# Two transformer layers on one core: weights split in pieces, context handed over by features, and another order of slots in the second pass

## The reference, cut to what matters

```
# layer 0
t1 = layer_norm(x) ; x = x + attn(t1, t1, mask) @ Wo.T + bo
x  = x + (context @ Wg.T + bg)
x  = x + relu(layer_norm(x) @ W1.T + b1) @ W2.T + b2
# layer 1
x  = x + mha(layer_norm(x), layer_norm(x), causal)
y  = x + mha(layer_norm(x), context)
z  = layer_norm(y) ; out = y + relu(z @ w1 + b1) @ w2 + b2      # 16 heads of 16 features
```

## Time and profile before

| | us |
|---|---|
| median of 3 runs | 1629.85 (1628.0 to 1630.69) |
| the profiled execution, its own time | 1625.86 |
| its span | 1624.1 |

### The profile page before, as it was taken

One profiled execution on the slowest core, in us unless ns is written; L12 is line 12 of the kernel. 1 busy time (PEld: TensorE's weight loads), 2 busy tenths in 40 slices (PEclk: granted clock), 3 DMA queues, 4 the chain that ended last, 5 costly groups with the idle time before them and its releaser, 6 DMA issues.

```text
span 1624.1 us, 39350 instructions
## 1 busy us (share of the span) xinstructions
PE 1448.7 (89%) x13568; PEld 1184.2 (73%) x13568; DVE 1193.5 (73%) x3871; ACT 1033.5 (64%) x2089; POOL 835.1 (51%) x1125
## 2 busy tenths in 40 slices
PE   2799999999999999878887888888999999999986
PEld 2578888888888888765665656656777777777766
DVE  3788878888888887767777677787677776777642
ACT  3677777777777775555666656666666566665652
POOL 4455544545555565544434444545565555656533
PEclk8899999999999999989999999999999999999999
DMA  4554433443344443444454454554344433344200
GB/s 134 163 147 120 120 105 105 116 121 105 112 117 124 125 124 92 131 124 135 113 144 124 112 146 120 158 145 117 97 111 119 117 100 103 105 119 123 79 20 13
DMA packets 163605, 187.07 MB, mean 115 GB/s; under 512 B 15953, under 2 KB 140241, under 8 KB 163409
## 3 DMA queue, kind: packets, MB, share of 16 engines
q1 hardware_dynamic: 163408, 184.57, 40.1%
HBM read 125.78 MB, written 58.72 MB: 114 GB/s over the span
## 4 chain that ended last, share of the span: by engine, by line
PE 59%; ACT 15%; DVE 14%; issue 8%; POOL 2%; DMA 1%; SPq 1%; DVEq 0%; ACTq 0%; POOLq 0%
PE d_ps L451 23%; PE d_ps L713 8%; PE o_ps L587 8%; PE s_ps L509 6%; PE t_ps L523 6%; DVE prob L915 4%; ACT prob_t L761 4%; PE t_ps L557 3%; ACT q_stack L769 3%; PE m_ps L458 3%; ACT xt_hi L776 1%; ACT h_f L853 1%; DVE top L900 1%; DVE stats L921 1%; DVE q_part L1017 1%
## 5 line engine op out<-in xcount | busy, mean ns | idle before, releaser
L761 ACT ACTIVATE prob_t<-t_ps 128x384 f32<-128x384 f32 (+1 forms) x512 | 275.7, 550 | 354.8 <-PE t_ps L557 189.3
L509 PE MATMUL s_ps<-k_stack,q_stack 96*128 96x256 bf16 (+1 forms) x1536 | 288.9, 270 | 81.0 <-DVE top L915 50.1
L752 ACT ACTIVATE prob<-prob,neg_max 128x256 f32<-128x256 f32 x512 | 233.5, 509 | 115.3 <-DVE neg_max L915 113.1
L509 PEld LDWEIGHTS s_ps<-k_stack,q_stack 96*128 96x128 bf16 x1536 | 116.1, 99 | 175.9 <-issue 68.2
L557 PE MATMUL t_ps<-q_stack,k_stack 108*128 108x256 bf16 (+1 forms) x1024 | 205.5, 267 | 29.8 <-ACT prob_t L761 27.4
L1137 POOL TENSOR_TENSOR h_lo<-h_f,h_hi 128x512 fp32r<-128x512 f32 x128 | 164.9, 1288 | 119.8 <-DVE h_hi L1032 119.8
L915 DVE CUSTOM_DVE_ANT_0 prob<-s_ps,bias_sb 128x256 f32<-128x256 f32 x512 | 193.3, 418 | 30.3 <-PE s_ps L509 29.8
L900 DVE TENSOR_REDUCE top<-s_ps 128x2 f32<-128x512 f32 x256 | 172.6, 682 | 46.8 <-PE s_ps L509 43.3
L915 DVE CUSTOM_DVE_ANT_0 prob<-s_ps,causal 128x128 f32<-128x128 f32 (+1 forms) x512 | 157.4, 352 | 54.5 <-PE s_ps L509 52.9
L587 PE MATMUL o_ps<-prob_t,v_sb 128*17 128x256 f32 (+1 forms) x3072 | 195.4, 373 | 0.0
L451 PE MATMUL d_ps<-x2t_hi,w_hi 128*128 128x256 f32 x512 | 156.6, 306 | 15.3 <-ACT k_f L834 10.3
(11 more groups left out here) (127 smaller groups left out, 4051.2 us busy)
## 6 DMA issues: line engine op xcount, KB each, us to landing
parts<-q_part SPq DMA_DIRECT2D x96, 192.0 KB, 2.3
parts<-k_part SPq DMA_DIRECT2D x96, 192.0 KB, 2.3
q_stack<-parts SPq DMA_DIRECT2D x96, 192.0 KB, 3.3
k_stack<-parts SPq DMA_DIRECT2D x96, 192.0 KB, 3.3
q_stack<-parts SPq DMA_DIRECT2D x96, 128.0 KB, 3.1
k_stack<-parts SPq DMA_DIRECT2D x96, 128.0 KB, 3.2
ct_kept<-ct_hl SPq DMA_DIRECT2D x16, 512.0 KB, 3.5
x_in<-x_mid SPq DMA_DIRECT2D x32, 256.0 KB, 3.0
```

The costliest lines, as they stand in the source:

```text
L509: last = mm(s_ps[:, h % 2, q * S:q * S + n], q_stack[0:ROWS, t.par, head_of(t, h), q * P:(q + 1) * P], k_stack[0:ROWS, t.par, head_of(t, h ...
L752: last = nc.scalar.activation(prob[:, h % 4, q, :], prob[:, h % 4, q, :], ACT.Exp, bias=neg_max[:, h % 4, q:q + 1], scale=-1.0)
L761: nc.scalar.activation(prob_t[:, h % 8, 0:n], t_ps[:, h % 2, 0:n], ACT.Exp, scale=-1.0)\
```

## The change

**The start.** x of the first item goes first, then Wq, and the pieces of the first unit have semaphores of their own; `rows_sb` goes last, under its own semaphore, for which only its first users wait. ACT's eight writes move to step -1, slot 5, behind the first q and k.

**Weights in pieces.** Each unit is cast and subtracted in pieces of 512 columns, one in a slot, at the places in `PIECE_AT`. W1 and W2 of pass 0 go to slots 8 to 11 of steps 0 and 1 (they were whole in slots 3 and 12 of step 0). W1 and W2 of pass 2 go to slot 12 of steps 18 to 25 (they were whole in slots 9 and 14 of step 17).

**Context.** It is handed over by features, so that `c_in` is split as it lands; the flip, ACT's copy, and their events go.

**The order of slots** in steps called `mixed`: `prev`, `cur` and `nxt` are all in pass 1 or 2 and `old` has no MLP, which holds for steps 18 to 33. There the second part of k moves from slot 6 to 8, the first norm from slots 9, 10 and 12 to 8, 9 and 10, the flip of x from 13 to 12 (its eviction and `xt_lo` one slot earlier too), the projection of V from 10 to 11; and in slots 8 to 10 DVE takes the minimum first instead of last. In other steps these places are what they were.

```diff
+START = (WQ, WK, WV)
-UNIT_AT = {(-2, 14): (0,), (-1, 13): (1,), (0, 3): (2,), (0, 12): (3,),
-           (14, 12): (4,), (16, 13): (5,), (17, 9): (6,), (17, 14): (7,), (30, 12): (8,), (32, 13): (9,)}
+PIECES = tuple(len(w) if kind == "a" else 4 for kind, _, w in UNITS)
+PIECE_AT = {0: ((-1, 13), (-1, 14)), 1: ((0, 8), (0, 9), (0, 10), (0, 11)), 2: ((1, 8), (1, 9), (1, 10), (1, 11)),
+            3: ((14, 12), (14, 13), (14, 14)), 4: ((16, 13),), 5: ((18, 12), (19, 12), (20, 12), (21, 12)),
+            6: ((22, 12), (23, 12), (24, 12), (25, 12)), 7: ((30, 12), (30, 13), (30, 14)), 8: ((32, 13),)}
+GUARD_FIRST = (8, 9, 10)
+XF_AT = 12
+P2_AT = (5, 8)
+LN_AT, V_MIXED, W1_AT, FLIP_AT = ((9, 10, 12), (8, 9, 10)), {True: 10, False: 11}, ((5, 6, 7, 8), (5, 6, 7, 8)), (1, 1)
...
+        self.mixed = all(t and t.p in KEYED for t in (self.prev, self.cur, self.nxt)) and not self.w1
...
+            sp.dma_start(x_in[:, 0], tokens(x[0])).then_inc(x_landed.of(Task(0, 0)), 16)
+            start_weight(0)
             sp.dma_start(ident_sb[:, :], ident).then_inc(const_landed, 16)
             sp.dma_start(cols_sb[:, :], cols).then_inc(const_landed, 16)
-            sp.dma_start(rows_sb[:, :, :], rows.partition_broadcast(P)).then_inc(const_landed, 16)
+            start_weight(1)
+            start_weight(2)
+            sp.dma_start(rows_sb[:, :, :], rows.partition_broadcast(P)).then_inc(rows_landed, 16)
...
-                if h == 4 and has(st.prev, (0,)):
-                    pe.wait_ge(ctx_landed.of(st.prev), ctx_landed.after(st.prev))
...
-                    flip(m_ps, c_in).then_inc(ct_mm.sem, 1)
...
+                if h == 5 and st.s == -1:
+                    choose_rows()
...
             def slot(st, h):
+                if has(st.cur) and st.mixed and h in GUARD_FIRST:
+                    score_guard(st, h)
...
-                if h == 6 and has(st.nxt):
+                if h == st.p2_at[1] and has(st.nxt):
                     dve.wait_ge(k_r.sem, k_r.after(st.nxt))
                     v.tensor_copy(k_part[:, 1], k_f[:, :, :]).then_inc(k_p2.sem, 1)
...
-                    v.tensor_copy(ct_hi[:, :, :], tf_b[:, :, :]).then_inc(ct_h.sem, 1)
+                    v.tensor_copy(ct_hi[:, :, :], c_in[:, :, :]).then_inc(ct_h.sem, 1)
...
-                if has(st.cur):
+                if has(st.cur) and not (st.mixed and h in GUARD_FIRST):
                     score_guard(st, h)
...
+                if (st.s, h) in UNIT_AT:
+                    u, n = UNIT_AT[st.s, h]
+                    if n == 0:
                         dve.wait_ge(unit_landed, 16 * (u + 1))
                         unit_users_done(dve, u)
-                        _, place, hi, _ = unit_io(u)
-                        v.tensor_copy(hi, place).then_inc(unit_hi, 1)
+                    place, hi, _ = piece_io(u, n)
+                    v.tensor_copy(hi, place).then_inc(unit_hi, 1)
```

More of the change, by code:

```diff
@@ L104, in __init__ @@
         self.prev, self.old, self.older = at(-1), at(-2), at(-3)
+        self.w1 = bool(self.old) and self.old.p in MLP
+        self.mixed = all(t and t.p in KEYED for t in (self.prev, self.cur, self.nxt)) and not self.w1
+        self.ln_at, self.w1_at, self.flip_at = LN_AT[self.mixed], W1_AT[self.mixed], FLIP_AT[self.mixed]
+        self.v_at = (V_MIXED[self.w1] if self.mixed else V_AT[self.nxt.p]) if self.nxt else None
+        self.v_first = self.v_at is not None and self.v_at < self.w1_at[1]
+        self.w2 = None
+        self.xf_at = XF_AT if self.mixed else 13
+        self.p2_at = P2_AT if self.mixed else (5, 6)
 def steps(body):
@@ L443, in _ @@
             mm = nc.tensor.matmul
-            pe.wait_ge(const_landed, 48)
+            pe.wait_ge(const_landed, 32)
             pe.wait_ge(setup, 4)
@@ L474, in bank_1_free @@
                     pe.wait_ge(v_done.sem, v_done.after(st.nxt))
-                if has(st.old, MLP) and not has(st.nxt, KEYED):
+                if has(st.old, MLP) and (st.v_first or not st.nxt):
                     pe.wait_ge(h_done.sem, h_done.after(st.old))
@@ L613, in slot @@
                     top_rows(st, t, ht // CH)
-                if h == 1 and has(st.old, MLP):
+                if h == st.flip_at and has(st.old, MLP):
                     pe.wait_ge(x2_hat_done.sem, x2_hat_done.after(st.old))
@@ L680, in slot @@
                     flip(m_ps, o_sb).then_inc(o2t_mm.sem, 1)
-                if has(st.nxt, KEYED) and h == V_AT[st.nxt.p]:
+                if has(st.nxt) and not st.v_first and h == st.v_at:
                     if has(st.old, MLP):
@@ L1043, in slot @@
                     statistics(x_in[:, st.nxt2.par], stats, ln_stats)
-                if h == 10 and has(st.nxt2):
+                if h == st.ln_at[1] and has(st.nxt2):
                     if st.nxt:
@@ L1165, in slot @@
                     sub(xt_lo[:, :, :], tf_a[:, :, :], xt_hi[:, :, :], xt_l.sem)
-                if h == 3 and has(st.old, MLP):
+                if h == st.flip_at + 2 and has(st.old, MLP):
                     rounded = x2t_h if st.old.p == 0 else x2t_f
@@ L1184, in slot @@
                     pool.wait_ge(ct_h.sem, ct_h.after(st.prev))
-                    sub(ct_lo[:, :, :], tf_b[:, :, :], ct_hi[:, :, :], ct_l.sem)
-                if 7 <= h <= 10 and has(st.old, MLP):
-                    n = h - 7
+                    sub(ct_lo[:, :, :], c_in[:, :, :], ct_hi[:, :, :], ct_l.sem)
+                if h - 2 in st.w1_at and has(st.old, MLP):
+                    n = st.w1_at.index(h - 2)
                     pool.wait_ge(h_h.sem, h_h.after(st.old, n + 1))
                     sub(h_lo[:, 2 * n:2 * n + 2, :], h_f[:, n % 2], h_hi[:, 2 * n:2 * n + 2, :], h_l.sem)
+                if h == 10 and st.s == -1:
+                    pool.wait_ge(rows_landed, 16)
+                    g.tensor_tensor(rows_sb[:, R_BO, :], rows_sb[:, R_BO, :], rows_sb[:, R_BG, :], ALU.add)\
+                        .then_inc(causal_made, 1)
+                    pool.wait_ge(causal_made, 6)
                 if h == 10 and has(st.prev, (0,)):
```

181 lines of the change are left out of this document (100 added, 81 removed).

## The result

The change took the median from 1630.27 to 1566.29 us, a ratio of 0.961 (95% interval 0.9588 to 0.9632). The forecast was 1570. The profiled execution took 1565.11, its span is 1563.3, so the spans differ by 60.8 where the sum had 60.2.

What follows compares the result with a forecast made beforehand. TensorE was taken to bound steps 2 to 14 and nearly the third pass, no engine alone steps 19 to 33. Terms summed to -60.2 from 1625.9, so 1565.7; the median 4.0 above gave 1570, range 1548 to 1594.

Steps and rivals of the forecast that it cites:

- Start, -5.5: Before the first scores: first eviction at 10.7 instead of 16.2, saving 5.5 us; bounds -3.3 and -7.
- Steps 0 and 1, -8: First two steps: W1 and W2 in pieces, -5.5 in step 0, -2.3 in step 1; bounds -3 and -10.
- Context by features, -6.6: Steps 2 to 16: four transposes go, 0.44 a step in 15 steps; -3.3 if half returns as a wait.
- Steps 17 and 18, -12.5: Both big weight splits go: -5.5 in step 17, -7 in step 18; bounds -8 and -14.
- Pieces in slot 12, +2.4: Steps 18 to 25: each W1 or W2 piece of the last pass costs VectorE 0.3, together 2.4 us more.
- Rival B: Steps 18 to 25: the pieces hold VectorE for the subtraction's 1.16 instead of 0.3, +7, 1577; chance 0.15.
- Reordered steps, 19 to 33, -30: Second pass: short k_part cast, earlier norm and minima first save 2.0 a step in 15 steps; bounds -9 and -51.
- Rival C: Steps 19 to 33: the clock stays up and the denser steps lose their dips, 10 less, 1560; chance 0.15.
- A: Second pass: VectorE bounds the steps, so only 0.6 a step is saved, 21 less gain, 1591; chance 0.17.
- E: Second pass: k_part slips 5.5, the stacks come late and the kernel gets slower, 1648; chance 0.03.
- D: Start and step 0: the start's gain is eaten by the mask's wait and added casts, +8, 1578; chance 0.10.
- best case of -90: Whole kernel: all terms at their most favourable bounds together, 90 us less, 1540; called unlikely.

Runs made afterwards that it cites:

- e8: The change with W2's first-pass pieces in slots 2, 3, 7, 13 of step 1 and later-pass third weight pieces in the next step's slot 1: 1562.39 us.
- e1: The change with all slot changes of steps 18 to 33 undone and the rest kept: 1603.6 us, ratio 0.9843.
- e13: The kernel before the change, with matmuls that nothing reads put in four TensorE waits of steps 18 to 33: 1621.32 us, ratio 0.995.
- e3: The change with only k's second part moved back from slot 8 to slot 6: 1603.77 us, ratio 0.9833.
- e11: The kernel of e3 with 14 matmuls that nothing reads at the end of slots 6 and 7 of steps 18 to 33: 1574.84 us, ratio 0.9671.
- e10: The change with q's second part moved from slot 5 to slot 6 in steps 18 to 33: 1557.4 us, ratio 0.9565.

## Why the prediction was right, step by step

*Start, -5.5.* It was 3.3, at the lower bound given. VectorE began at 5.72, only 0.9 sooner and not 2.2, and the table load stood behind the flip as expected. The eviction came 4.3 sooner. Of this 0.6 went in the first 24 matmuls of the projections: in both kernels they start at 1.2 GHz (0.41 a matmul, 0.28 at 2.4 GHz), but before the clock rose at 22.9, inside the 24 (4.84 in all), and after only at their end, 20.2 (5.47). (The level is read from the matmuls' length: PEclk says 1.00 for this stretch, but the trace has no clock record ahead of that rise.) The eight writes end at 29.06, and item 1's eviction still waits 0.22 for its flip: they are hidden, as priced. The first scores wait for `k_stack`'s transfer (4.07).

*Steps 0 and 1, -8.* They gave 2.6, below the lower bound of 3. Step 0 gave 4.1 of the 5.5. The failing part is step 1. The wait of 2.26 for the mask is gone, as priced at -2.3, but the four pieces that take the split's place hold GpSimd up to 86.5 and TensorE waits 2.45 for `ot_lo`. I had costed them at nothing against one big cast. e8 gives 2.7 of it back.

*Context by features, -6.6.* It gave 4.7. Steps 2 to 14 lost 0.43 each, as priced, but for step 5 with 0.1 (5.4 in all); but step 16 lost only 0.1, and step 15 grew by 0.8 from the third piece of its weights, which e8 took away.

*Steps 17 and 18, -12.5.* 16.3, beyond the bound of 14. Both steps lost clock dips with their waits (0.91 and 0.78 to 1.00), which the sum left out. How much of the 16.3 is clock was not measured; without the reordering (e1) step 18 takes 23.6, so the splits and the clock behind them bring 7.6 of its 8.7.

*Pieces in slot 12, +2.4.* Steps 22 to 25 with a piece take 22.5, step 28 without one 22.3: 0.2 each, 1.6 in all, if the piece is all that sets them apart. Rival B did not come: beside these pieces VectorE has only the transposing copy (0.44) and minima of at most 0.42.

*Reordered steps, 19 to 33, -30.* 33.7, with seven of the pieces inside, so some 35 for the reordering. The clean step went from 24.4 to 22.5, 1.9 where 2.0 was priced. Its parts: `k_part` 0.7 (0.6 priced), the norm and flip 1.4 (1.44 priced), the minima and V nothing. Rival C came true inside this term: one step with a dip instead of ten, 8 of the 33.7 by e13, so the order itself gave 26 and, with the pieces, 27 of its 30. Steps 31 to 33 are where it gave less (25.6, 23.6 and 24.2; before 24.3, 25.8 and 25.0). So mechanism and size were right, but what I had called a bonus of 10 with a chance of 0.15 belongs to the mechanism: the order that takes the waits away gives the clock back too, and in e3, where one of the two places stays as it was, the clock costs 28.9.

*Rivals A and E.* The steps are not VectorE-bound (A), and the stacks were in time (E): in the profile after no scores at a step's head wait for them. D came in part, in step 1. The tail came out 1.6 longer (85.9); without any edit there it is between 84.0 and 87.4 in the profiled runs of the experiments, so no cause is sought.

The sum was 0.6 from the measured difference of the spans because errors cancel: the start, steps 0 and 1 and the context gave 9.5 less than priced (2.2 + 5.4 + 1.9) and the tail 1.6, against 3.8 more in steps 17 and 18, 5.8 in steps 19 to 33 with their pieces and 1.6 in step 34. That is luck in the sum; the two large terms were right within a third. In the prediction's best case of -90 the context stands at 8, for which it gives no row.

## What to carry to other kernels

Where TensorE idles several times in a short stretch, price the wait twice: what it takes itself, and what the lower clock may take from the work behind it. Whether the clock drops has to be read from the profile, since the same two waits came with and without a drop here. Filling such waits with matmuls that nothing reads shows in one run how much of a stage is clock; in both kernels where it was tried it also gave that time back. A cast that lies beside a GpSimd subtraction lasts until just behind its end; look for a slot where GpSimd is idle, and when a large operation is cut in pieces, see what each piece stands ahead of on GpSimd.

## What the runs showed of the hardware

- Waits of 1.08 and 1.10 whose ends are 3.9 apart leave the clock at 1.00 (step 24 of after). With waits of 1.08 and 0.98 whose ends are 1.6 apart, 14 of 16 steps of e3 are at 0.93 or below, but only 10 of steps 19 to 33 of the kernel before, which has the same two; with both filled (e11) none is. The steps of e3 take 23.2 at 1.00 (step 19; 25.1 in step 33), 24.0 to 24.4 at 0.93 and 0.86 (but 25.2 in step 32 and 29.0, at 0.76, in step 31), and 25.7 to 25.8 at 0.80.
- A cast of `q_part` or `k_part` that begins during a GpSimd subtraction ends 0.27 to 0.29 after the subtraction's end, wherever it began. The rows of e3, GpSimd first:

```profile
828.89 1.15 POOL L1177 TENSOR_TENSOR q_part<-q_f,q_part 128x512 bf16<-128x512 f32 x1 [0.36 <-DVE q_part L1055]
...
829.29 1.04 DVE L1060 CAST k_part<-k_f 128x512 bf16<-128x512 f32 x1
```

The subtraction ends at 830.04 and the cast at 830.33. For `q_part` it is 817.28 after 817.01 in the profile after, and 795.01 after 794.73 in e10. In the profile after, 73 of the 75 casts of `q_part` and `k_part` that begin so end 0.28 to 0.29 behind the subtraction; the other two begin in its last 0.05. This is the rule weighed in the prediction (the Trainium skill's "SBUF — State Buffer", section "SBUF: two separate sides"), and the trace agrees: the cast is held until the other instruction is through, and then takes little.
